# W2, the carried part of o and the update of s2 in fp32 on halves of TensorE's array, instead of zero-padded split pairs on the whole array

## The reference

```python
q, k = rope(hs @ Wq.T), rope(hs @ Wk.T);  v = hs @ Wv.T;  g = hs @ Wg.T
s   = clip(hs @ Ws1.T @ Ws2.T + bs2, -32, 32)          # 64 slots a head
es  = exp(s);  enz = exp(-cumlogsumexp(s))
A   = tril(q k^T * scale);  ok = enz * (A @ es)
p   = softmax(ok over the slots) * enz
W2  = tril(p @ es^T);       o = W2 @ v
out = (o * rsqrt(mean(o*o) + EPS) * g_norm * g*sigmoid(g)) @ Wo.T
x   = layernorm(x + out);   x = layernorm(x + x @ (W*scale).T + bias)
```

## Time and profile before

| | |
|---|---|
| median of 3 runs | 1559.19 us (1558.36 to 1561.25) |
| profiled execution, span | 1558.6 us (its time outside the span is not listed) |
| PE busy | 1510.6 us, 97%, 8720 records |
| PEld busy | 1280.0 us, 82% |
| DVE busy | 1038.4 us, 67% |
| POOL busy | 648.5 us, 42% |
| ACT busy | 625.5 us, 40% |
| DMA | 109.88 MB, mean 70 GB/s |

### The profile page before, as it was taken

The page is one execution under the profiler, slowest core; times in us unless marked ns, Lnnn a source line. Parts: engine busy times, 40 slices in busy tenths (PEclk is TensorE's granted clock), DMA queues, the critical chain, the costliest instruction groups (busy, mean ns, idle before and its releaser), DMA issues.

```text
span 1558.6 us, 24100 instructions
## 1 busy us (share of the span) xinstructions
PE 1510.6 (97%) x8720; PEld 1280.0 (82%) x8720; DVE 1038.4 (67%) x1840; ACT 625.5 (40%) x1235; POOL 648.5 (42%) x641
## 2 busy tenths in 40 slices
PE   7899999999899999999899999999999999999988
PEld 3788888888788888888788888888888888888866
DVE  4766657567676766667866666666776675667667
ACT  5433334335333333333433433333533333433346
POOL 2444343444443443444433434334444443444345
PEclk9999999999999999999999999999999999999999
DMA  8420212013221101202311120212222011201123
GB/s 321 173 78 23 71 44 71 22 62 114 71 71 45 63 29 39 75 27 86 133 49 45 37 77 22 71 44 92 83 68 75 29 64 44 71 22 45 62 81 122
DMA packets 51444, 109.88 MB, mean 70 GB/s; under 512 B 5376, under 2 KB 15616, under 8 KB 46976
## 3 DMA queue, kind: packets, MB, share of 16 engines
q1 hardware_dynamic: 49088, 104.94, 20.1%
q10 hardware_dynamic: 2304, 4.20, 0.7%
HBM read 86.84 MB, written 26.21 MB: 73 GB/s over the span
## 4 chain that ended last, share of the span: by engine, by line
PE 70%; issue 9%; DVE 8%; ACT 6%; POOL 5%; DMA 1%; POOLq 0%; SPq 0%; DVEq 0%; ACTq 0%
PE bank_qv L859 21%; PE bank_kg L859 20%; PE bank_t L873 5%; PE bank_s L977 3%; PE bank_a L859 3%; PE bank_a L896 3%; PE bank_o L1046 3%; PE bank_s L979 3%; PE bank_c L1058 2%; PE bank_o L859 2%; PE bank_s L859 2%; DVE pT_lo L628 2%; ACT pT_hi L475 2%; ACT batch_raw L475 2%; DVE pair_pT_lo L628 1%
## 5 line engine op out<-in xcount | busy, mean ns | idle before, releaser
L395 POOL TENSOR_TENSOR hs_lo<-hs_raw,hs_hi 128x512 fp32r<-128x512 f32 x64 | 81.5, 1274 | 362.5 <-ACT hs_hi L475 362.5
L859 PE MATMUL bank_qv<-w_hi,hs_hi 128*128 128x512 f32 x512 | 210.2, 411 | 12.8 <-issue 6.6
L859 PE MATMUL bank_kg<-w_hi,hs_hi 128*128 128x512 f32 x512 | 208.2, 407 | 1.0 <-DVE rope_b L648 1.0
L859 PE MATMUL bank_qv<-w_hi,hs_lo 128*128 128x512 f32 x512 | 204.4, 399 | 0.0
L859 PE MATMUL bank_qv<-w_lo,hs_hi 128*128 128x512 f32 x512 | 204.2, 399 | 0.0
L859 PE MATMUL bank_kg<-w_hi,hs_lo 128*128 128x512 f32 x512 | 202.2, 395 | 0.0
L859 PE MATMUL bank_kg<-w_lo,hs_hi 128*128 128x512 f32 x512 | 202.2, 395 | 0.0
L475 ACT ACTIVATE oT_hi<-bank_t 128x512 fp32r<-128x512 f32 x65 | 38.8, 597 | 331.6 <-PE bank_t L873 331.6
L400 POOL TENSOR_TENSOR q_rot<-rope_a,rope_b 128x512 f32<-128x512 f32 x64 | 82.3, 1286 | 187.7 <-DVE rope_b L648 187.7
L628 DVE TENSOR_TENSOR pT_lo<-bank_t,pT_hi 64x256 fp32r<-64x256 f32 x128 | 54.0, 422 | 123.3 <-ACT pair_pT_hi L475 122.2
L390 POOL TENSOR_TENSOR v_lo<-batch_raw,ws_low 128x512 fp32r<-128x512 f32 x64 | 82.6, 1290 | 115.0 <-ACT ws_low L475 114.8
(11 more groups left out here) (190 smaller groups left out, 3757.3 us busy)
## 6 DMA issues: line engine op xcount, KB each, us to landing
w_raw<-w_groups SPq DMA_DIRECT2D x32, 1024.0 KB, 4.9
x_scratch<-part SPq DMA_DIRECT2D x65, 256.0 KB, 2.0
hs_raw<-hs_cols SPq DMA_DIRECT2D x64, 256.0 KB, 2.7
part<-x_scratch SPq DMA_DIRECT2D x64, 256.0 KB, 3.1
batch_raw<-hs_cols SPq DMA_DIRECT2D x4, 1024.0 KB, 7.7
u_part<-u_scratch SPq DMA_DIRECT2D x64, 64.0 KB, 2.4
w_raw<-x_scratch SPq DMA_DIRECT2D x16, 256.0 KB, 2.7
x_scratch<-hs_rows SPq DMA_DIRECT2D x1, 3840.0 KB, 16.0
```

Source lines behind the costliest of these rows:

```text
L395: pool.tensor_tensor(hs_lo[slot][:, :], hs_raw[slot][:, :], hs_hi[slot][:, :].bitcast(F32), ALU.subtract).then_inc(hs_lo_made, 1)
L859: mm = pe.matmul(dst, x, y, start=start and n == 0, stop=stop and n == 2, **kw)
```

## The change

W2, the carried part and the s2 update become fp32 matmuls, one per head. For W2 and the carried part each takes the 64 partitions of its head (even heads 0 to 63, odd heads 64 to 127) as the contraction; the two parities write to different banks: bank_s and bank_o become one tensor bank_wo of 1024 columns, W2 in the first half of each bank, o in the second. The s2 update has the 64 columns of es of one head as weights, all 128 partitions as contraction, and writes to partitions 0 to 63 or 64 to 127 of bank_s2 by parity. The hi and lo tensors of pT, pair_pT, esT, v and s2 go, with the instructions that made them; pT, esT and s2 are plain fp32 copies by ACT. The carried part is issued behind W2, ahead of o = W2 @ v, which adds to it. The output product moves from bank_o to bank_a, so the scores, not o, wait for part_made; W2 waits for s_clipped, because its bank holds the slots of the next chunk. DVE's mask of W2, ACT's square and DVE's gating read both banks by parity. In the last phase bank_s and bank_a change places.

```diff
-        s2_hi, s2_lo = sb("s2_hi", HG * DV, F32R), sb("s2_lo", HG * DV, F32R)
+        pT, s2 = sb("pT", H), sb("s2", H)
...
+        bank_wo = ctx.enter_context(nc.psum_tensor("bank_wo", [P, 1024], F32))
+        bank_s, bank_o = bank_wo[:, 0:512], bank_wo[:, 512:1024]
+        slots_acc = bank_wo[:, H:2 * H]
+        s2_acc = bank_s2[:, 0:H]
+
+        def w2_of(h):
+            start = 512 * (h % 2) + P * (h // 2)
+            return bank_wo[:, start:start + P]
+
+        def o_of(h):
+            start = 512 * (h % 2) + H + P * (h // 2)
+            return bank_wo[:, start:start + P]
+
+        def paired(bank_half):
+            return bank_wo[:, :].rearrange("p (e k r x) -> p e k r x", e=2, k=2, x=P)[:, :, bank_half, :, :]
+
+        def by_parity(ap):
+            return ap.rearrange("p (r e x) -> p e r x", e=2, x=P)
...
-                act.wait_ge(pT_mm, i)
-                copy(of_pair(pT_hi[:, :], 0, P), per_head(bank_t[0:64, 0:H], 2))
-                copy(of_pair(pT_hi[:, :], 1, P), per_head(bank_t[64:128, 0:H], 2))
-                copy(pair_pT_hi[:, :], bank_t[:, 0:H]).then_inc(pT_hi_made, 1)
-                if left:
-                    v_split((c + 1) % 2, n)
+                from_bank(pT[:, :], bank_t[:, 0:H], pT_mm, i, pT_made)
...
-                    act.wait_ge(s2_mm, carried(u, c))
-                    copy(of_pair(s2_hi[:, :], 0, DV), of_pair(bank_s2[:, :], 0, DV))
-                    copy(of_pair(s2_hi[:, :], 1, DV), of_pair(bank_s2[:, :], 1, DV)).then_inc(s2_hi_made, 1)
+                    from_bank(s2[:, :], s2_acc, s2_mm, carried(u, c), s2_made)
...
-                dve.wait_ge(pT_hi_made, i)
-                minus_pair(pT_lo, pT_hi, P, lambda half: per_head(bank_t[64 * half:64 * half + 64, 0:H], 2))
-                minus_hi(pair_pT_lo[:, :], bank_t[:, 0:H], pair_pT_hi[:, :]).then_inc(pT_lo_made, 1)
...
                 for h in range(HG):
-                    mm = product(bank_o[:, :], cols((oT_hi, oT_lo), P * h, P), cols((wo_hi, wo_lo), D * h, D),
+                    mm = product(bank_a[:, :], cols((oT_hi, oT_lo), P * h, P), cols((wo_hi, wo_lo), D * h, D),
                                  start=h == 0, stop=h == HG - 1)
                 mm.then_inc(out_mm, 1)
 
-                pe.wait_ge(pT_lo_made, i)
-                for r in range(HG // 2):
-                    mm = product(bank_a[:, 2 * P * r:2 * P * r + 2 * P], cols((esT_hi, esT_lo), P * r, P),
-                                 cols((pT_hi, pT_lo), 2 * P * r, 2 * P))
+                pe.wait_ge(pT_made, i)
+                if left:
+                    pe.wait_ge(s_clipped, n)
+                for h in range(HG):
+                    rows, at = slice(64 * (h % 2), 64 * (h % 2) + 64), slice(P * (h // 2), P * (h // 2) + P)
+                    mm = pe.matmul(w2_of(h), esT[rows, at], pT[rows, at], start=True, stop=True)
+                if c:
+                    pe.wait_ge(s2_made, carried(u, c - 1))
+                    for h in range(HG):
+                        rows, at = slice(64 * (h % 2), 64 * (h % 2) + 64), slice(P * (h // 2), P * (h // 2) + P)
+                        mm = pe.matmul(o_of(h), pT[rows, at], s2[rows, at], start=False, stop=False,
+                                       skip_group_check=True)
                 mm.then_inc(w2_mm, 1)
...
                 pe.wait_ge(w2_masked, i)
-                pe.wait_ge(part_made, i)
                 for h in range(HG):
                     head = slice(P * h, P * h + P)
-                    mm = pe.matmul(bank_o[:, head], masked[:, head], v[now][:, head], start=h == 0, stop=c == 0,
+                    mm = pe.matmul(o_of(h), masked[:, head], v[now][:, head], start=False, stop=True,
                                    skip_group_check=True)
-                if c:
-                    pe.wait_ge(s2_lo_made, carried(u, c - 1))
-                    for r in range(HG // 2):
-                        mm = product(bank_o[:, 2 * DV * r:2 * DV * r + 2 * DV],
-                                     cols((pair_pT_hi, pair_pT_lo), P * r, P), cols((s2_hi, s2_lo), 2 * DV * r, 2 * DV),
-                                     start=False, skip_group_check=True)
                 mm.then_inc(o_mm, 1)
...
-                    pe.wait_ge(v_lo_made, i)
-                    for r in range(HG // 2):
-                        mm = product(bank_s2[:, 2 * DV * r:2 * DV * r + 2 * DV],
-                                     cols((es_hi[now], es_lo[now]), P * r, P),
-                                     cols((v_hi[now], v_lo[now]), 2 * DV * r, 2 * DV),
-                                     start=c == 0 and r == 0, skip_group_check=True)
+                    for h in range(HG):
+                        rows, at = slice(64 * (h % 2), 64 * (h % 2) + 64), slice(DV * (h // 2), DV * (h // 2) + DV)
+                        mm = pe.matmul(s2_acc[rows, at], es[now][:, M * h:M * h + M], v[now][:, DV * h:DV * h + DV],
+                                       start=c == 0 and h < 2, stop=True, skip_group_check=True)
                     mm.then_inc(s2_mm, 1)
                 if left:
+                    pe.wait_ge(part_made, i)
                     scores(n)
```

More of the change, by code:

```diff
@@ L99, in gated_slot_attention_block @@
         k_rot = [sb(f"k_rot{s}", F) for s in range(2)]
-        v_lo = [sb(f"v_lo{s}", F, F32R) for s in range(2)]
         es_hi = [sb(f"es_hi{s}", H, F32R) for s in range(2)]
         es_lo = [sb(f"es_lo{s}", H, F32R) for s in range(2)]
-        esT_hi, esT_lo = sb("esT_hi", H, F32R), sb("esT_lo", H, F32R)
+        esT = sb("esT", H)
         enz = sb("enz", H)
@@ L380, in _ @@
                 pool.memset(t[:, :], 1.0).then_inc(ones_set, 1)
-            for t in (wo_hi, wo_lo, pT_hi, pT_lo, s2_hi, s2_lo):
+            for t in (wo_hi, wo_lo):
                 pool.memset(t[:, :].bitcast(F32), 0.0).then_inc(zeroed, 1)
@@ L668, in lo @@
                 minus_hi(dst, src, hi).then_inc(made, 1)
[L670 to L677, removed]
             def clip(n):
                 dve.wait_ge(s_mm, n)
-                dve.tensor_scalar(s_clip[:, :], bank_s[:, 0:H], CLAMP, -CLAMP, ALU.min, ALU.max).then_inc(s_clipped, 1)
+                dve.tensor_scalar(s_clip[:, :], slots_acc, CLAMP, -CLAMP, ALU.min, ALU.max).then_inc(s_clipped, 1)
             def make_gate(slot, n):
@@ L691, in make_enz, with mask_a, mask_w2 @@
                 dve.reciprocal(enz[:, :], cums).then_inc(enz_made, 1)
-            def mask(mm, n, made):
-                dve.wait_ge(mm, n)
+            def mask_a(n):
+                dve.wait_ge(a_mm, n)
                 dve.tensor_tensor(per_head(masked[:, :]), per_head(bank_a[:, :]), over_heads(keep), ALU.mult
-                                  ).then_inc(made, 1)
+                                  ).then_inc(a_masked, 1)
+            def mask_w2(n):
+                dve.wait_ge(w2_mm, n)
+                dve.tensor_tensor(by_parity(masked[:, :]), paired(0),
+                                  keep.unsqueeze(1).unsqueeze(1).broadcast_to([P, 2, 2, P]), ALU.mult
+                                  ).then_inc(w2_masked, 1)
             split_u(0)
@@ L804, in step @@
                 dve.wait_ge(part_in[c % 2], (u * (CB // 2) + (c // 2 + 1)) * 16)
-                dve.tensor_tensor(part[c % 2][:, :], bank_o[:, :], part[c % 2][:, :], ALU.add).then_inc(part_made, 1)
+                dve.tensor_tensor(part[c % 2][:, :], bank_a[:, :], part[c % 2][:, :], ALU.add).then_inc(part_made, 1)
                 if not left:
                     tick(2, 2)
-                mask(w2_mm, i, w2_masked)
+                mask_w2(i)
                 if not left:
                     tick(3, 3)
-                if left:
-                    esT_split(n)
                 if last and c == 2:
@@ L820, in step @@
                 dve.wait_ge(oT_mm, i)
[L821 removed]
+                dve.tensor_tensor(by_parity(o_gated[:, :]), paired(1), by_parity(gate[c % 2]), ALU.mult
+                                  ).then_inc(o_gated_made, 1)
                 dve.tensor_reduce(sum_sq[:, :], per_head(o_sq[:, :]), AX.X, ALU.add).then_inc(sq_summed, 1)
@@ L827, in step @@
                 if left:
[L828 to L832, removed]
+                    mask_a(n)
                 if c == 0:
@@ L998, in step @@
                     pe.wait_ge(u_in[nxt], (u * 2 + ((c + 1) // 2 + 1)) * 16)
-                    pe.matmul(bank_s[:, 0:H], u_part[nxt][:, :], ws2_cols(g, last and c == CB - 1), start=True,
+                    pe.matmul(slots_acc, u_part[nxt][:, :], ws2_cols(g, last and c == CB - 1), start=True,
                               stop=True).then_inc(s_mm, 1)
```

61 lines of the change are left out of this document (23 added, 38 removed).

## The result

The changed kernel takes 1537.44 us in the median of 4 runs (1534.6 to 1538.59), the kernel before 1558.78 beside it: a ratio of 0.986, 95% interval 0.9846 to 0.9875. It is 1.4% faster, 21.3 us. The forecast was 49 us. The four runs spread by 4 us, and their mean granted clock goes with it: 0.996 in the quickest, 0.992 in the slowest.

What follows compares the result with a forecast made beforehand. PE's record pace bounds the kernel, plus a hole before W2 each step. From 1558.6 us: -0.6 for records and waits, -72 for overlapping halves, +22 for switches gives 1508, stated as 1510 us; range 1485 to 1580.

Steps and rivals of the forecast that it cites:

- records and waits at a full pace: PE's W2, carried part, s2 and esT_lo wait, without overlap of halves: -12.8 + 8.6 + 5.8 - 2.2 = -0.6 us.
- The hole at W2: PE's idle time before W2, waiting for pair_pT_lo, mean 0.28 us a step, 18 us in all, would go.
- item 1: W2, 64 times: eight fp32 records at 0.89 us replace 1.09 us including the hole; -12.8 us.
- The overlap: 1280 new PE records on array halves run at 0.056 instead of 0.112 us: 72 us less.
- loads rival: Weight loads go one at a time; W2 and carried part stay at 0.105 us, only s2 gains; 1553 us, chance 0.17.
- no-overlap rival: Each fp32 record waits for the one before, whichever half; 1580 to 1616 us with switches paid; chance 0.28.
- The switches: 224 PE changes between whole array and halves, taken at 0.10 us each: 22 us more.
- the upper bound: Per switch, the array empties and starts anew: 0.26 us, 58 us for 224.
- "I put 0 for the move": Moving the carried part ahead of the WG projection costs 0; without PE's cover, 0.7 us of mask a step.
- s2: The s2 update, 48 times: 0.77 us becomes 0.89 without overlap (+5.8 us), 0.45 with it.
- esT_lo: PE's single wait for esT_lo, 2.2 us, goes: -2.2 us at most.

Runs made afterwards that it cites:

- e7: As e2, but W2 and the carried part of all four heads computed on partitions 0 to 63 (output not the reference's); 1566.17 us, ratio 1.0047.
- e1: Changed kernel with heads of W2, carried part and s2 issued in the order 0, 2, 1, 3; 1539.7 us, ratio 0.9869.
- e3: As e2, but the carried part issued behind o, where it stood before, making two more switches in 48 steps; 1536.82 us, ratio 0.9853.
- e2: Changed kernel, but ACT copies hs_hi right behind pT, so POOL makes hs_lo earlier; 1521.05 us, ratio 0.9751.
- e5: Kernel before the change, with ACT's copy of hs_hi moved early, behind the copies of pT; 1552.67 us, ratio 0.996.
- e8: Changed kernel without the early hs_hi copy, carried part back behind o only in steps with c = 3; 1529.27 us, ratio 0.9804.
- e4: As e2, but the s2 update is the old split pairs on the whole array, with v_hi and v_lo; 1519.0 us, ratio 0.9741.
- e6: As e2, but the s2 update issued right behind the carried part, three switches instead of four in 48 steps; 1515.63 us, ratio 0.9725.

## Why the prediction was right in direction and wrong in size

The prediction's sum was -0.6 (records and waits at a full pace), -72 (overlap), +22 (switches), with 0 for moving the carried part.

- **The hole at W2** (18 us in item 1): right. The detour is off the chain, and W2 starts 0.31 us behind the last record of the output product (621.84 to 622.15), where 0.23 was its pace; I count the rest to the switch. PE nowhere waits for the copy of pT.
- **The overlap** (72 us): right, and its pace is the one that was put in, 0.056 us. The loads rival and the no-overlap rival fell with the 0.45 us of the carried part; e7 gives 45 us for 896 records, 0.050 each. How it comes about I first had wrong: the prediction let the second record of one head run beside the first of the next, and e1 showed that heads need not alternate. (The load rival's upper end, 1567, was also wrongly added: with 0.26 us a switch it is 1558.6 - 27.4 + 58 = 1589.)
- **The switches** (22 us): the first term that was mis-sized. I took 0.10 us, the restart alone, from the bounds 0 and 0.26. It is 0.165 (e3), so 224 of them cost 37 us, 15 more than forecast. I had reckoned that the weight load of the next record would be queued already; but ahead of W2 PEld stood idle 0.35 us each time, and W2's first load starts together with its first record at 622.15. The time stands on both sides of an edge, in the group (0.65 and 0.59 instead of 0.45) and in what comes behind it (the scores 1.09 instead of 0.89), as the upper bound had it, at two thirds of its size. The Trainium skill, TensorEngine Tiling (Array Packing), Key Properties, says that a change of the tiling mode drains the TensorE; the trace agrees in that every change costs time, 0.33 us for a pair, but not at the price of the full emptying (0.26 each): W2's first record starts 0.31 us behind an output record that is listed with 0.39.
- **"I put 0 for the move"** of the carried part: the step that failed. I checked who would wait for the mask of W2 at the new place, but not what the carried part had covered at the old one: PE's wait for hs_lo in the step with c = 3, of which 0.3 us showed. The row of that wait (12 times, 3.5 us) was among the waits of before, and the prediction doesn't use it. I even named that step as the one with the tightest cover, and looked only at o's norm there. The price is 10 us. The distances between the first ok records give it directly: W2 and s2 gained 0.26 us in a step with c = 0 (21.61 to 21.35), the carried part another 0.25 with c = 1 or 2 (23.20 to 22.69), but with c = 3 the 0.51 became a loss of 0.16 (21.93 to 22.09): 0.67 us in each of 15 passages. e2 and e5 show that 0.52 of it is PE's wait for hs_lo; the other 0.15 stays in e2, most likely the wait for kT. e8 shows that the place of the carried part is the cause.
- **s2**: by the prediction's terms it was to gain 48 x (0.77 - 0.45) = 15 us less 10 for its switches. With the measured switches (16 us) nothing is left, and e4, with the old s2, is 2 us faster: this is part of the same mis-sized term.
- **esT_lo** (2.2 us at most): mis-sized the other way. PE's wait there fell from 2.2 to 0.6 us, and with it went the stretch at half the clock behind it: 4.4 us. The prediction read the clock from the page's slices, where that stretch doesn't show.

With the measured sizes of the switches and of the lost cover the sum is -0.6 - 72 + 37 + 10 = -26 us, against the measured 21.3. That it comes this near is partly luck: by the distances between the ok records all the steps together give only about 16 us, and 4.4 come from ahead of the first step. Of what the steps lack against the sum, 1.6 us are at the passages between groups of heads (from the first ok record of the step with c = 3 to that of the next step, 26.96, 27.02 and 22.46 us became 28.30, 27.61 and 22.10). In the first of them the granted clock was 0.5 for 3.4 us before and for 6.8 now:

```profile
414.70:418.10 3.40, 3.40 (x10) 2.62 (x9) 0.00 (x0) 0.00 (x0) 0.00 (x0) 0.50 0.00 0
```

```profile
404.00:410.80 6.80, 3.62 (x9) 2.85 (x10) 0.00 (x0) 0.00 (x0) 1.25 (x2) 0.50 0.01 2
```

That is no mark of the change: in e4 it was 3.4 us in the first passage (26.29 us long) and 6.8 in the second (27.32). The rest, some 6 us or under 0.1 a step, stays open.

## What to carry to other kernels

A group of matmuls on part of the array must be long enough to pay for its two switches: here eight records on halves save 0.45 us and the switches take 0.33 (0.40 where nothing is covered), so a lone group gains little, two groups side by side gain about 0.5, and a group that replaces something cheaper than itself gains nothing. Put the groups together, and don't look for a clever order of heads inside them. When an instruction moves on the engine that bounds, look at both places: a wait of 0.3 us in the list of waits means that the work ahead of it is cover for its releaser, and here what left that stretch bought nothing. Look at the granted clock in narrow windows behind each long wait: here a wait that was 1.6 us longer cost 4.4.

## What the runs showed of the hardware

Two fp32 matmuls on different row halves start together (two records begun within 0.02 us), the next two 0.22 us later at the start of a stretch and 0.112 us later within it; on one half they follow at 0.112 us. PE found that overlap also where neighbours in program order were on one half (0.65 us for W2 in either order), at a small loss in the next group (0.54 instead of 0.45). The records don't name their head, so the order in which PE took them can't be read. A direct switch from row halves to column halves saved 0.11 us in the time and 0.14 in the chain against going by the whole array (e6). Behind a wait of 2.2 us the granted clock was 0.51 for 6.9 us; behind one of 0.6 us at the same place it stayed at 1.00.
